# The second normalization of the rows, batch by batch: written by VectorE before, by GpSimd after

## What is computed

```python
x = x + tanh(g_xattn) * attention(ctx, layernorm(x), mask, ...)   # called x1 in the kernel
z2 = (x - mean) / sqrt(var + eps)                                 # the second norm, row by row
bids = sigmoid(z2 @ conf_w.T + conf_b) * wealth                   # routing: two experts for each row
x = x + tanh(g_ffn) * combine(bids, experts(z2))
```

## Time and profile before

| what | value |
|---|---|
| median of 3 runs | 1436.77 us (1435.43 to 1438.32) |
| the profiled execution | 1435.85 us, its span 1434.3 us |
| mean granted TensorE clock | 0.989 |
| PE busy | 1351.1 us (94%) |
| DVE busy | 1023.5 us (71%) |
| ACT busy | 934.8 us (65%) |
| POOL busy | 488.2 us (34%) |

### The profile page before, as it was taken

The page is one execution under the profiler, slowest core; times in us unless marked ns, Lnnn a source line. Parts: engine busy times, 40 slices in busy tenths (PEclk is TensorE's granted clock), DMA queues, the critical chain, the costliest instruction groups (busy, mean ns, idle before and its releaser), DMA issues.

```text
span 1434.3 us, 41525 instructions
## 1 busy us (share of the span) xinstructions
PE 1351.1 (94%) x13880; PEld 969.2 (68%) x13880; DVE 1023.5 (71%) x2528; ACT 934.8 (65%) x1932; POOL 488.2 (34%) x659
## 2 busy tenths in 40 slices
PE   2999999999999999999999979999999999999996
PEld 1466666666666666666665657688878778887784
DVE  4688888888888888888888776566556654444442
ACT  5687878787787878878787765566656663333331
POOL 4423322433433334334333143433344333222221
PEclk9999999999999999999999979999999999999998
DMA  4010101111111111111112146433376753112461
GB/s 119 27 42 26 42 23 29 52 40 49 34 53 30 41 46 39 49 33 53 31 33 96 41 129 196 107 98 93 98 211 178 228 152 94 31 31 35 120 203 16
DMA packets 56913, 109.26 MB, mean 76 GB/s; under 512 B 10832, under 2 KB 34768, under 8 KB 56720
## 3 DMA queue, kind: packets, MB, share of 16 engines
q0 software_dynamic: 23712, 55.71, 15.2%
q1 hardware_dynamic: 32160, 49.86, 11.2%
q10 hardware_dynamic: 848, 1.07, 0.3%
HBM read 69.16 MB, written 37.45 MB: 74 GB/s over the span
## 4 chain that ended last, share of the span: by engine, by line
PE 70%; DVE 10%; ACT 6%; issue 6%; DMA 5%; SPq 1%; POOL 1%; POOLq 0%; DVEq 0%; ACTq 0%
PE fP L1542 19%; PE yP L1542 10%; PE uP L1542 10%; PE gP L1542 10%; PE simP L1590 5%; PE ptP L1600 4%; PE tP L1542 3%; PE oP L1542 3%; DVE ms L1036 3%; DVE pT L1042 2%; DMA out<-ysb,xt 2%; PE aP L1773 2%; DVE ao L1054 1%; ACT z L732 1%; PE fP L1558 1%
## 5 line engine op out<-in xcount | busy, mean ns | idle before, releaser
L1542 PE MATMUL fP<-zTs,ws 128*128 128x112 f16 (+1 forms) x1536 | 220.3, 294 | 8.7 <-DVE zTs L1378 5.3
L1542 PE MATMUL fP<-ws,zTs 128*128 128x512 f16 x768 | 186.8, 379 | 0.5 <-DVE kT L1026 0.2
L1036 DVE CUSTOM_DVE_ANT_0 ms<-simP,madd,sim_undo 112x488 f32<-112x488 f32 x256 | 183.9, 720 | 3.3 <-PE simP L1590 1.3
L769 ACT ACTIVATE pr<-ms,nmax 112x488 f32<-112x488 f32 x256 | 179.0, 699 | 3.3 <-DVE nmax L1036 0.5
L1042 DVE SCALAR_TENSOR_TENSOR pT<-ptP,pT 122x448 f16<-122x448 f32 x256 | 157.8, 616 | 28.0 <-ACT pT L776 27.3
L1542 PEld LDWEIGHTS fP<-zTs,ws 128*128 128x128 f16 x1536 | 109.8, 99 | 99.7 <-issue 34.9
L1542 PE MATMUL yP<-W,aT 128*128 (+1 forms) x1512 | 175.4, 273 | 1.8 <-DVE aT L1414 1.8
L1542 PEld LDWEIGHTS yP<-W,aT 128*128 128x128 f16 x1512 | 147.6, 98 | 32.8 <-issue 2.5
L1408 DVE SCALAR_TENSOR_TENSOR act_h<-uP,consts,sg 128x512 f32<-128x512 f32 x126 | 94.5, 750 | 103.1 <-ACT sg L899 102.7
L776 ACT ACTIVATE pT<-ptP 122x448 f16<-122x448 f32 x256 | 137.8, 538 | 40.8 <-PE ptP L1600 39.7
L899 ACT ACTIVATE sg<-gP,consts 128x512 f32<-128x512 f32 x126 | 86.5, 686 | 114.6 <-PE uP L1542 114.4
(11 more groups left out here) (233 smaller groups left out, 2496.2 us busy)
## 6 DMA issues: line engine op xcount, KB each, us to landing
raw<-wffn POOLq DMA_DIRECT2D x36, 512.0 KB, 6.9
split_experts<-W POOLq DMA_DIRECT2D x12, 1024.0 KB, 10.0
W<-split_experts SPq DMA_DIRECT2D x16, 768.0 KB, 7.9
xc<-ctxt SPq DMA_DIRECT2D x32, 375.0 KB
xt<-routed_rows POOLq DMA_DIRECT2D x63, 129.0 KB, 2.4
raw<-wffn SPq DMA_DIRECT2D x12, 512.0 KB, 9.5
routed_rows<-padrows SPq DMA_DIRECT2D x8, 645.0 KB, 7.9
xl<-x SPq DMA_DIRECT2D x32, 112.0 KB
```

The costliest lines, as they stand in the source:

```text
L769: nc.scalar.activation(pr[h % 2][:, :], ms[h % 2][:, :], ACT.Exp, bias=nmax[p][:, h:h + 1], scale=-1.0, accum_out=rsum[p][:, h:h + 1]).the ...
L1036: nc.vector.tensor_tensor_reduce(out=ms[h % 2][:, :], in0=simP[h % 2][0:S, 0:NK], in1=madd[p][:, :], scale=sim_undo[0:S, 0:1], scalar=3.0e ...
L1542: last = nc.tensor.matmul(o, lhs(k, a), rhs(k, c), start=n == 0, stop=n == len(todo) - 1)
```

## The change

For 30 of the 32 batches (b-1 = 0 to 29) the second norm is no longer an instruction of VectorE in slot 6 but one of GpSimd, directly behind the power that ends `rstd1`. For the last two batches it stays on VectorE, in the tail. `residual` of the next batch, which overwrites `mv1`, now waits until z2 has been written (`s_z2`) where it waited for the inverse deviation (`s_rs1`).

```diff
@@ gpsimd
+            def norm2(b, g):
+
+                pool.wait_ge(s_rs1, b + 1)
+                need(pool, s_zcopy, b - 3)
+                nc.gpsimd.tensor_scalar(z2[g][:, :], x1[g % 2][:, :], mv1[:, 0:1], rs1[:, 1:2], ALU.subtract, ALU.mult).then_inc(s_z2, 1)
+
...
                 if holds(b, 1, B - 1):
                     rstd1(b - 1)
+                if holds(b, 1, B - 2):
+                    norm2(b - 1, (g - 1) % 4)
                 if b == B - 1:
                     scatter(q - 1, 1)
@@ vector, residual
                 dve.wait_ge(s_bn1, b + 1)
-                need(dve, s_rs1, b)
+                need(dve, s_z2, b)
                 apart(dve)
                 nc.vector.bn_aggr(mv1[:, :], bn1[:, :]).then_inc(s_mv1, 1)
@@ vector, body
-                    if h == 6 and holds(b, 1, B - 2):
-                        norm2(b - 1, (g - 1) % 4)
                     route_some(2)
```

## The result

| what | before | after |
|---|---|---|
| median | 1436.19 us (6 runs, 1433.34 to 1438.32) | 1444.38 us (6 runs, 1441.85 to 1447.5) |
| ratio to before | 1 | 1.006, interval 1.0042 to 1.0078 |
| the profiled execution (span) | 1435.85 us (1434.3) | 1444.63 us (1443.0) |
| mean granted TensorE clock | 0.989 | 0.991 |

The change costs 0.6%, about 8.2 us, where a gain of 7.8 us was forecast. Rival 3 is what happened in the main: GpSimd's norm is slow, and PE waits for it. The page's line of busy time, the one that answers to the earlier trace rows, hardly tells it: VectorE has lost its 30 instructions, GpSimd gained 38 us, PE is the same.

A forecast was written before the change was run, and what follows sets the result against it. PE, busy 94% of the span, was taken to bound the kernel, idling near the norm for VectorE; 20 x 0.32 + 6 x 0.18 + 0.3 = 7.8 us less gave 1429.0 us against the median, 8-in-10 range 1426.5 to 1435.0.

The forecast's parts named there:

- Rival 3: Ahead of the transposes of z2: GpSimd's norm is slow and PE waits, kernel slower, 1442.4 us at 1.3 us; chance 0.06.
- D: Length of one norm instruction on GpSimd, 256 columns: taken as 0.65 us, between 0.47 and 0.92.
- the point of 1.11: Length in us of GpSimd's norm at which the forecast gain is gone, PE waiting ahead of the transposes.
- 13.3 - 29 s: Gain in us over all batches if PE's chain binds everywhere; s is what the norm's length exceeds 0.65 us by.
- the lower bound of the gain: Gain over all batches with the norm at 0.92 us, transposes 0.27 us later still: 4.7 us.
- Small terms: Norm 0.18 us behind the power, transposes 0.10 behind the norm, simP no sooner than 0.98 behind the transposes.
- VectorE's 0.32 us: Everything behind z in VectorE's list, pT and nmax too, comes 0.32 us earlier in a batch.
- the one near 771 us: Batch with expert-ordering steps between pT and nmax, where VectorE's side binds by far: 0.3 us gained.
- rival 1: Routing steps in 20 batches wait for GpSimd's norm, 0.15 us each: +1.6 us, 1438.4 us; chance 0.08.
- Cost nothing: Scatters and next mask queued behind the norm on GpSimd come 0.85 us later, at no cost.
- Rival 2: Another wait in the batch, at ScalarE or VectorE, takes the 0.32 us: whole 1436.8 us, half 1433; chance 0.08.

The follow-up runs named there:

- the first experiment: Kernel before, with two rounds of eight GpSimd instruction forms added behind its last work, no other engine running: the norm's form took 1.23 us.
- the later transposes: Changed kernel, with PE's transposes of z2 moved behind the last transposes of probabilities and the values of slot 7: 1431.05 us, 0.9962.
- the spread one: Changed kernel, with scatters spread, one pair per batch from batch 8 on, ahead of the first inverse deviations: 1442.91 us, 1.0042.
- the kernel before with all scatters ahead: Kernel before, norm on VectorE, with all scatters of a batch moved ahead of the inverse deviations on GpSimd's list: 1445.69 us, 1.0063.
- the changed kernel with all scatters ahead: Changed kernel, with all scatters of a batch moved ahead of the inverse deviations on GpSimd's list: 1440.17 us, 1.0027.
- without eps: Changed kernel, with the addition of eps ahead of the power left out, so z2 comes 0.41 us earlier: 1432.98 us, 0.9982.
- longer wait: Changed kernel, with a one-column GpSimd instruction of the same form added between the power and the norm: 1460.78 us, 1.0167.

## Why the prediction was wrong

**The step that failed is D**, "I take 0.65, between copy and L499", with the bounds of 0.47 and 0.92 around it. It measured 1.24 us in the kernel and 1.23 alone. What went wrong in it is plain from the first experiment: I ranked the form by its inputs (one tensor, contiguous, so near the copy). On this engine a scalar form takes 0.85 us with one constant, 0.92 with one per-row scalar and 1.23 with two; the copy takes 0.40 and the two-tensor product 0.72. The mask was the nearest row: it is the same instruction with one operation, at 2.55 ns a column. I took its price as an upper bound, but it has one operation and the norm has two. The 0.92 is just what one operation with a per-row scalar takes; a bound would have had to add the second (0.3 us). With that the 0.92 would have been 1.2, past the point of 1.11 at which rival 3 decides.

**Rival 3's formula was right.** 13.3 - 29 s with s = 1.24 - 0.65 = 0.59 gives 3.8 us more (its terms add up to 13.24, and those of the lower bound of the gain to 4.6, not 4.7; neither matters), and the kinds of batches, as measured ahead of the scatters, add up to 4.0. It had a chance of 0.06 because the bound was too low. Its example (D = 1.3, 1442.4 us) lies 2 us under the 1444.4 measured, and the wait makes only some 4 of the 8.2 us.

**Small terms.** The norm starts 0.12 us behind the power, not 0.18; PE starts 0.05 behind the norm, not 0.10; simP comes 1.08 behind the transposes, not 0.98, since oP to simP takes 0.45 here. Together 0.01 us.

**VectorE's 0.32 us** was right where no routing step runs beside the norm (0.30 measured, with the later transposes) and too large, by 0.1 to 0.2 us, where one does and the norm begins 0.24 us ahead of it. Of the 8.6 us that 26 batches of 0.32 and the one near 771 us would have made, 5.4 were kept. The Trainium skill (SBUF — State Buffer, Who interferes with whom) has the later of two such instructions wait for the whole of the other; the step at 549.20, with two SBUF inputs, would then have waited until 549.96. It took 0.21 us in place of that, 0.48 us into the norm. So rival 1 did not occur. The 0.1 to 0.2 us are small beside the wait of PE.

**"Cost nothing" for what is queued behind the norm** was wrong by some 3 us. Shown: in traces with late signals, moving the pair away from behind the norm takes 2.8 of them away (the changed kernel against the spread one), and the one batch of the spread kernel that has such a pair takes 3.1 us more than before. Shown too: PE's wait for the norm is neither needed for late signals (the kernel before with all scatters ahead has them and loses 1.2 us in each fourth batch) nor enough (the changed kernel with all scatters ahead has a pair at that same place, and loses 0.27). Not shown: what makes a trace one with late signals, and what holds PE's signals until the scatters have been issued. The last step of 1.6 us, between 7.1 at the last batch and 8.7 in the span, lies in the second stage, which the change doesn't touch, and is within the spread of the runs.

**Rival 2** (the gain swallowed) did not occur either: with the later transposes the gain of the first stage, 5.5 us at the last batch, is whole in the median (5.5).

## What to carry to other kernels

Before moving an elementwise instruction to an engine for which no row has its form, measure that form by itself, with its number of operations and scalars: the kind of input says little. An instruction that moves off a busy engine must still be in time for its reader: with the reader's chain written out (here 2.49 us from the power to simP) the break-even length is known, and where it isn't met, the reader can be moved instead. One place later in PE's list turned 0.6% slower into 0.4% faster, with the norm as slow as before. And before a difference between two traces is put down to the order of instructions, look for it at a place where both kernels are alike: here the late signals were there too.

## What the runs showed of the hardware

- GpSimd, 112 partitions, 256 float32 columns: copy 0.40 us, two-tensor product 0.72, one operation with a constant 0.85, with a per-row scalar 0.92, two operations with constants 1.09, with per-row scalars 1.23 (0.80 at 128 columns, 0.39 at one). VectorE did the last in 0.40, so GpSimd is 3.1 times slower at it.
- The two to four small VectorE steps of a batch take 0.10 to 0.16 us more together, up to pT, when such an instruction begins 0.24 us ahead of them (changed kernel, later transposes), and nothing more when it begins 0.66 us ahead (without eps) or 0.26 us behind their first (longer wait); in the last case it took 1.41 us itself beside four of them. In none of these does one stop for the other.
- In nine of fourteen traces PE's signals that fall due while GpSimd issues a pair of indirect DMAs, or just behind it, reach VectorE and ScalarE late, and mostly 0.5 to 0.7 us after the end of the second DMA's record: ScalarE's aoT waits 0.76 us and more where it waits 0.68 in the five others. PE need not have waited for GpSimd. The cost goes by what is due: nothing ahead of the inverse deviations, 2.8 us in all behind the norm, 1.2 us in a batch with four DMAs in a row. The mechanism is open.
- TensorE's granted clock fell from 2.4 to 1.2 GHz (1.00 to 0.50) for some 3.4 us behind a pause of 1.53 us, which cost 1.7 us, as much again as the pause.
